# Softmax maxima from one-bank score pieces with the mask in the product, and the last output projections moved behind attention

## The chip, the cores and the metric

The kernel runs on one core of a Trainium2 chip. The metric is the device time of one launch in microseconds (us), lower is better. The engines are PE (TensorE, matmuls), DVE (VectorE), ACT (ScalarE), POOL (GpSimd) and SP (SyncE, which only issues DMAs here).

## The reference, cut to what matters

```python
xn = layernorm(x)                                  # x: 4 x 1024 x 512
q, k, v = proj(xn, Wq, bq), proj(xn, Wk, bk), proj(xn, Wv, bv)   # 16 heads of 32
s = q @ k.T / sqrt(32)                             # per batch and head, 1024 x 1024
s = where(key > query, -inf, s) - slope[h] * |key - query|
attn = softmax(s) @ v;   out1 = attn @ Wo.T + bo
g, u = split(xn @ w1[e].T);  y = (silu(g) * u) @ w2[e].T         # 8 experts, top 2 of each token
return x + out1 + moe(y, softmax gate weights)
```

## The kernel before, in words

A function `plan()` writes out by hand one order of steps (`o.steps`). Every engine's program runs through that list and emits its own steps, so each engine works its part strictly in that order, and semaphores order the engines among each other.

Attention runs over 16 groups (`G`), a batch times four heads each, and 40 units (`u`) in a group. A unit is one head's scores for 256 queries and up to 256 keys: matmuls at L1248 to L1253, kept transposed (keys on partitions) in one of two PSUM banks `C`, then an exponential on ACT (L1842). Four units make a quad, whose probabilities go through POOL's addition (L1946) and PE's products with V (L1266) and with ones (L1276 to L1279, the sums). A quarter `q` of the queries ends with `osb` (ACT), `fold` (a small DMA), `rcp` (DVE), `unfold` (a small DMA), `bc` (PE, L1288), `a32` (DVE) and `aT` (POOL).

The exponential needs each row's maximum beforehand. It comes from a first computation of the scores, with queries on partitions (`pre`, L1223), whose row maximum DVE takes (`mx`, L1652). There are 32 items a group, one for each 128-query tile `j` and head `h`, each 128 (j+1) keys wide. The DVE instruction adds a table `rel` (the distance, and -1e30 behind the diagonal) and reduces in one go. Items with j > 3 fill both banks A and B (1024 columns, two matmuls of up to 512 columns), the others one of A and C. The maxima are turned (`mtr`, L1235), copied (`mcp`, ACT) and written by a small DMA (`mrow`) into an extra row of the stacked operands, so that the second scores come out with the maximum subtracted. That stacked operand has 96 rows of q and k pieces (`stack`, 12 DMAs a group, L1041), 9 rows of positions (`place`) and the row of the maxima. Group G's items are placed from unit 40 G - 32 on.

Between the units `plan()` places filler with due times, for which units earn credit: projections of the next group (L1192, L1209), layer norm, the gate, and the output projections `proj_o(b, i)` (L1300, 12 matmuls of 512 columns each; 8 a batch). These used two further banks, T, in turn, whichever was free for the longest (`borrow`, `give`). The last batch's projections are placed from unit 604 on, due by unit 686 at the latest.

SP also issues the loads of the expert weights in six windows (`win`, L1126). Each waits for the buffers it overwrites; window 3 waits for the last products with V and the last sums. After unit 640 and the projections the mixture of experts follows (L1338, L1353, L1369): 71 slots of 128 tokens, the first of which needs the gate weights of windows 0 to 3.

Of the kernel before, what the change touches and what calls it, by code (L numbers as in the profile page):

```python
# [8 lines left out]
P = 128  # L9
B, S, E = 4, 1024, 512  # L10
NT = B * S // P
H, D = 16, 32
NG = 4
# [34 lines left out]
MAXIMA = ([(j, h) for j in (0, 1) for h in range(4)] + [(j + 2 * k, h) for j in (2, 3) for h in range(4) for k in (0, 1)]  # L48
          + [(j, h) for j in (6, 7) for h in range(4)])
# [3 lines left out]
C_ID, C_U, C_ONE, C_REL, C_IOTA, C_SLOPE, C_ALPHA, C_TAU, C_POS, C_END = (  # L53
    0, 128, 256, 384, 1408, 1416, 1432, 1436, 1436 + NSLOT, 1564 + NSLOT)
# [3 lines left out]
BND, SW, IW, SQ, IQ, SG, IG, CV, SQQ, CK, T0, CO, NQ = range(6, 19)  # L58
# [88 lines left out]
def plan():  # L147
# [131 lines left out]
    def maxima(n):  # L279
        G = n // 32  # L280
        j, h = MAXIMA[n % 32] if G else (n // 4, n % 4)
        key = "pre", G, j, h
        if j > 3:
            banks = ["A", "B"]
        else:
            banks = ["C"] if (G and j > 1) or h % 2 else ["A"]
        o.bank[key] = "C" if banks == ["C"] else "A"
        o.emptied[key] = [s for x in banks for s in o.tenant.get(("P", x), [])]
        add(*key)
        add("mx", G, j, h)  # L290
        for x in banks:
            o.tenant["P", x] = [("mx", G, j, h)]
        if h == 3 and j % 2:
            def row():
                take_m("mtr", G, j // 2)
                add("mtr", G, j // 2)

                def rest():
                    add("mcp", G, j // 2)
                    o.give(("mtr", G, j // 2), ("mcp", G, j // 2))  # L300
                    add("mrow", G, j // 2, sem=f"mrow{j // 2}", inc=16)

                later.append(rest)

            at(now[0] + 2, row)
# [277 lines left out]
    for cost in start:  # L583
        if cost:
# [6 lines left out]
            if i == 15:  # L591
                stack(0, 0)
                add("place", 1, sem="pos0", inc=16 * 5)
                add("otop")
# [6 lines left out]
    add("place", 2, sem="pos1", inc=16 * 5)  # L601
# [35 lines left out]
    for b in range(B):  # L637
# [23 lines left out]
    for n in range(32 * GROUPS):  # L661
        G, k = n // 32, n % 32
        due.setdefault(U0 + k // 2 if G == 0 else TG * G - 32 + k * 5 // 4, []).append(n)
# [60 lines left out]
    o.tenant["S", 0] = o.tenant["P", "A"] + o.tenant["P", "B"]  # L724
    o.tenant["S", 1] = o.tenant["C", 0] + o.tenant["C", 1]
    o.tenant["Y", 0], o.tenant["Y", 1] = o.tenant["O", 0], o.tenant["P", "C"]
# [60 lines left out]
def build(nc, ctx, T):  # L787
# [49 lines left out]
    down = sb("down", [P, 1], F32)  # L837
# [12 lines left out]
    rel = cF[:, C_REL:C_REL + S]  # L850
# [29 lines left out]
    junk, to = place(to, [P, S], F32)  # L880
# [3 lines left out]
    zeros = junk[:, 0:E]  # L884
    spill = [junk[:, k * 512:(k + 1) * 512].bitcast(BF16) for k in range(2)]
# [5 lines left out]
    mneg, to = place(to, [P, 2, 32], F32)  # L891
# [27 lines left out]
    PB = TB  # L919
    CB = [GU[1][:, 0:512], GU[1][:, 512:1024]]  # L920
    MXB = {"A": GU[0], "C": MB}
# [76 lines left out]
    def sync(sp):  # L998
        on = Once(sp)
        sp.dma_start(idh, T["cH"][:, 0:P]).then_inc(sems["csth"], 16)  # L1000
        for step in o.steps:
# [41 lines left out]
            elif kind == "place" and key[0]:  # L1043
# [8 lines left out]
            elif kind == "mrow":  # L1052
# [8 lines left out]
            elif kind == "fold":  # L1061
# [3 lines left out]
            elif kind == "unfold":  # L1065
# [33 lines left out]
            elif kind == "win":  # L1099
# [15 lines left out]
                elif key[0] == 4:  # L1115
                    on.wait_ge(*at("mx", GROUPS - 1, 7, 3))
# [17 lines left out]
    def tensor(pe):  # L1134
        on = Once(pe)
        reg = {}
        for step in o.steps:
# [76 lines left out]
            elif kind == "pre":  # L1214
                G, j, h = key
                w = P * (j + 1)
                z = MXB[o.bank[step]]
                for s in o.emptied[step]:
                    on.wait_ge(*at(*s))
                on.wait_ge(*at("stack", G // NG, G % NG, h))  # L1220
                for n0 in range(0, w, 512):
                    n1 = min(w, n0 + 512)
                    tp = pe.matmul(z[:, n0:n1], stk[G % 2][0:96, h, 0, j * P:(j + 1) * P], stk[G % 2][0:96, h, 1, n0:n1],  # L1223
                                   start=True, stop=True)
                tp.then_inc(sems["pre"], 1)
            elif kind == "mtr":
# [4 lines left out]
                for j in (2 * q, 2 * q + 1):  # L1231
                    for h in range(4):
                        on.wait_ge(*at("mx", G, j, h))
                for j in range(2):
                    tp = pe.transpose(z[0:4, j * P:(j + 1) * P], mneg[:, G % 2, 8 * q + 4 * j:8 * q + 4 * j + 4], idf)  # L1235
# [140 lines left out]
    def vector(dve):  # L1376
# [135 lines left out]
        then(dve.memset(down[:, :], -MDOWN))  # L1512
        for step in o.steps:
# [67 lines left out]
            elif kind == "scales" and key[0] == 4:  # L1581
                scales(MG, SG, IG, -80)
                then(dve.tensor_scalar(col(T0), col(SQQ), col(SQ), None, ALU.mult))
# [4 lines left out]
                then(dve.tensor_scalar(sel, sel, col(SQ), None, ALU.mult))  # L1588
                dve.tensor_scalar(rel, rel, col(T0), None, ALU.mult).then_inc(sems["scales"], 1)
# [51 lines left out]
            elif kind == "mx":  # L1641
                G, j, h = key
                w, m = P * (j + 1), 4 * j + h
                if G > 1:
                    on.wait_ge(*at("mtr", G - 2, j // 2))
                elif G == 0:
# [460 lines left out]
```

## Time and profile before

| | |
|---|---|
| median of 3 runs | 1655.44 us (1653.47 to 4988.74) |
| the profiled execution | 1652.5 us, of which the span of its instructions is 1650.7 us |
| granted PE clock, mean | 0.954 of full |
| PE busy | 1454.1 us, 88% |
| DVE, ACT, POOL busy | 922.4, 704.0, 875.4 us |

Busy time of PE tells when it had something in flight, not at what rate. The line PEclk of the page is the clock that PE was granted, in tenths of full speed. Times of rows are counted from the span's start. A bracket at a row's end is idle time of the engine just ahead of it, and what ended it.

### The profile page before, as it was taken

Reading aid. Unit: us, or ns where it says so; the run is one execution under the profiler, and the core shown is the slowest. Engines: PE = TensorE matmul, PEld = TensorE weight load, DVE = VectorE, ACT = ScalarE, POOL = GpSimd, SP = SyncE. Lnnn points to the kernel's source line nnn. Section 1 sums busy time; section 2 is a strip of 40 time slices with the busy share of each in tenths; the row PEclk is TensorE's granted clock in tenths of the full one; section 3 lists DMA queues with packets and bytes.
Section 4 is the critical chain, followed back from the end, with each engine's and each line's share of the span. In section 5 each row is a group of like instructions: output and inputs, shape, how many; then the busy total and the mean of one; then the engine's idle time right before and its main releaser. Section 6 shows DMA issues by size and latency. Waiting matters only on the chain. (4 is left out here: it accounts for less than half of the span.)

```text
span 1650.7 us, 35380 instructions
## 1 busy us (share of the span) xinstructions
PE 1454.1 (88%) x13147; PEld 845.5 (51%) x13147; DVE 922.4 (56%) x2128; ACT 704.0 (43%) x1179; POOL 875.4 (53%) x756
## 2 busy tenths in 40 slices
PE   4779988888997889998889889897579999999995
PEld 2345545454553554555555455553246655566663
DVE  7656775665667556657568886762134333333332
ACT  5134555444565554655655434354212222222221
POOL 4124446345356553645546535555425777767774
PEclk9789989999999999999899999998889999999997
DMA  7233541426433245433242511105786888888894
GB/s 256 64 86 105 154 129 56 116 74 178 124 120 91 87 142 156 130 108 107 74 113 84 152 28 32 40 2 186 233 252 102 135 134 137 130 121 138 142 145 49
DMA packets 189366, 194.45 MB, mean 118 GB/s; under 512 B 104953, under 2 KB 139001, under 8 KB 189074
## 3 DMA queue, kind: packets, MB, share of 16 engines
q1 hardware_dynamic: 161778, 152.84, 34.7%
q0 software_dynamic: 26128, 37.24, 13.7%
q8 instruction: 112, 1.84, 0.5%
q10 hardware_dynamic: 1296, 2.11, 0.3%
q14 instruction: 52, 0.43, 0.1%
HBM read 93.66 MB, written 53.74 MB: 89 GB/s over the span
## 5 line engine op out<-in xcount | busy, mean ns | idle before, releaser
L1842 ACT ACTIVATE arena<-S,psl 128x512 f32<-128x512 f32 (+1 forms) x640 | 403.4, 643 | 420.8 <-PE S L1250 215.4
L1652 DVE CUSTOM_DVE_ANT_0 arena<-S,cF,down 128x768 bf16<-128x768 f32 (+6 forms) x324 | 306.2, 945 | 203.5 <-PE S L1223 161.7
L1946 POOL TENSOR_TENSOR arena<-arena 128x1024 f32<-128x1024 f32 (+1 forms) x160 | 316.2, 1977 | 168.8 <-ACT arena L1842 168.6
L2000 POOL DMA_INDIRECT out<-arena x142 | 221.9, 1563 | 107.0 <-ACT arena L1895 49.6
L1338 PE MATMUL S<-arena 128*128 x1704 | 265.7, 312 | 1.2 <-issue 1.2
L1223 PE MATMUL S<-arena 96*128 96x512 f16 (+2 forms) x580 | 159.3, 348 | 76.1 <-DVE arena L1652 74.0
L1338 PEld LDWEIGHTS S<-arena 128*128 128x128 f16 x1704 | 166.3, 98 | 97.5 <-issue 2.0
L1192 PE MATMUL T<-arena 128*128 128x512 f16 x768 | 203.6, 393 | 2.0 <-DVE arena L1568 0.8
L1248 PE MATMUL S<-arena 106*128 106x256 f16 x640 | 179.9, 282 | 13.3 <-ACT arena L1842 12.7
L1266 PE MATMUL O<-arena 128*32 128x256 f32 (+1 forms) x2560 | 165.3, 378 | 0.5
L1652 DVE CUSTOM_DVE_ANT_0 arena<-M,cF,down 128x384 bf16<-128x384 f32 (+3 forms) x188 | 110.8, 589 | 90.6 <-PE M L1223 80.9
L1935 POOL TENSOR_TENSOR arena<-arena 128x512 f16<-128x512 f32 x64 | 77.3, 1208 | 142.5 <-DVE arena L1623 138.6
L1761 DVE COPY arena<-T 128x512 f16<-128x512 f16 x71 | 30.2, 425 | 213.7 <-PE T L1353 198.5
L1879 ACT ACTIVATE arena<-S,sc 128x352 f32<-128x352 f32 x71 | 39.4, 555 | 210.9 <-PE S L1338 192.0
L1266 PEld LDWEIGHTS O<-arena 128*32 128x32 f32 x2560 | 80.0, 115 | 66.5 <-issue 23.2
L1223 PEld LDWEIGHTS S<-arena 96*128 96x128 f16 x580 | 44.8, 99 | 134.4 <-DVE arena L1652 108.6
L1209 PE MATMUL T<-arena 128*128 128x128 f16 x1536 | 107.4, 221 | 6.3 <-DVE arena L1636 5.2
L1192 PEld LDWEIGHTS T<-arena 128*128 128x128 f16 x768 | 73.2, 100 | 75.2 <-issue 12.7
L1209 PEld LDWEIGHTS T<-arena 128*128 128x128 f16 x1536 | 96.2, 99 | 22.4 <-DVE arena L1636 8.0
L1956 POOL CAST arena<-arena 128x256 f16<-128x256 f32 x64 | 27.7, 433 | 148.3 <-DVE arena L1662 148.3
L1250 PE MATMUL S<-arena 106*128 106x256 f16 x384 | 104.8, 275 | 0.0
L1300 PE MATMUL T<-arena 128*128 128x512 f16 x384 | 100.7, 389 | 3.8 <-ACT arena L1849 2.0
(182 smaller groups left out, 2167.9 us busy)
## 6 DMA issues: line engine op xcount, KB each, us to landing
arena<-arena SPq DMA_DIRECT2D x192, 128.0 KB, 2.4
arena<-in_w1T SPq DMA_DIRECT2D x64, 352.0 KB, 3.5
arena<-in_x SPq DMA_DIRECT2D x64, 256.0 KB, 3.8
w_d<-arena SPq DMA_DIRECT2D x32, 352.0 KB, 2.8
arena<-w_d SPq DMA_DIRECT2D x16, 704.0 KB, 6.7
arena<-in_w2T SPq DMA_DIRECT2D x32, 256.0 KB, 3.0
out<-arena SPq DMA_DIRECT2D x32, 256.0 KB, 2.5
xn_d<-arena SPq DMA_DIRECT2D x24, 256.0 KB, 2.2
```

The costliest lines, as they stand in the source:

```text
L1192: tp = pe.matmul(z[:, :], wqkv[:, w_, c, f:f + P], xnT[:, a, c, half * 512:half * 512 + 512], start=(third == 0 and c == 0), stop=(third = ...
L1209: tp = pe.matmul(z[:, i * P:(i + 1) * P], xnT[:, a, c, k * P:(k + 1) * P], wqkv[:, w_, c, 2 * E + g * P:2 * E + (g + 1) * P], start=(n == ...
L1223: tp = pe.matmul(z[:, n0:n1], stk[G % 2][0:96, h, 0, j * P:(j + 1) * P], stk[G % 2][0:96, h, 1, n0:n1], start=True, stop=True)
L1248: pe.matmul(z[:, 0:2 * P], K[0], stk[G % 2][0:KROWS, h, 0, q0:q2], start=True, stop=False)
L1250: tp = pe.matmul(z[:, 2 * P:4 * P], K[1], stk[G % 2][0:KROWS, h, 0, q0:q2], start=False, stop=True)
L1266: tp = pe.matmul(OB[D * x:D * x + D, f:f + n], V[(G + 1) % 3][:, 2 * i + k, x * D:(x + 1) * D], PT[t % 3][:, x, c:c + n], start=(i == 0 an ...
L1300: tp = pe.matmul(z[:, :], aT[:, a, c, i * P:(i + 1) * P], wo[:, w_, c, :], start=(third == 0 and c == 0), stop=(third == 2 and c == 3))
L1338: tp = pe.matmul(y[:, i * 512:i * 512 + I], xT[:, s % XDEEP, 4 * a + c, :], weights[:, bass.ds(reg[s] + (w_ * NX * W1N + c * 2 * I + i * I ...
L1652: dve.tensor_tensor_reduce(spill[k % 2][:, 0:w], MXB[o.bank["pre", G, j, h]][:, 0:w], rel[:, S - w:S], down[:, 0:1], 3.0e38, ALU.add, ALU.min,
L1842: act.activation(PT[t % 3][:, h, 0:n], CB[o.bank["score", u]][:, 0:n], ACT.Exp, scale=psl[:, hh:hh + 1]).then_inc(sems["exp"], 1)
L1946: pool.tensor_tensor(PS[t % 2][:, :, f:f + n], PT[t % 3][:, :, f:f + n], PT[t % 3][:, :, c:c + n], ALU.add).then_inc(sems["add"], 1)
L2000: pool.indirect_dma_start(out=halves, out_offset=bass.IndirectOffsetOnAxis(row[:, part, s:s + 1].bitcast(U32), 0), in_=yo[:, s % YDEEP, c0 ...
```

## The change

The first scores are cut into 38 pieces a group, each of at most 512 columns (one bank): one head's tile over up to 512 keys, or the same stretch of two or four heads side by side. They come from the same pool as all other short-lived PSUM tenants, which now has five banks. The product now takes in the 9 rows of positions (105 rows), so that the distance is in it; pieces that reach the diagonal get one more matmul, 128 columns a head, which adds -2^30 behind the diagonal. DVE takes plain maxima over a piece of up to four heads; for j > 3 the second part is joined to the first. Items of group G are placed one a unit, from unit 40 G - 32 on. `rel` and its scaling go, and the constants shrink by 1024 columns.

The 8 output projections of the last batch are placed from unit 640 on. `place` is 2 DMAs instead of 5. In the last group `mrow`, `fold` and `unfold` are issued by ACT instead of SP.

```diff
+PIECES = [(0, (0, 1, 2, 3), 0, P), (1, (0, 1), 0, 2 * P), (1, (2, 3), 0, 2 * P)]
+PIECES += [(j, (h,), 0, P * (j + 1)) for j in (2, 3) for h in range(4)]
+for j in range(4, 8):
+    PIECES += [(j, (h,), 0, 4 * P) for h in range(4)]
+    n = 4 if j == 4 else 2 if j == 5 else 1
+    PIECES += [(j, tuple(range(h, h + n)), 4 * P, P * (j + 1)) for h in range(0, 4, n)]
...
-        self.since, self.owner = dict.fromkeys(range(2), 0), {}
+        self.since, self.owner = dict.fromkeys(range(5), 0), {}
...
     def maxima(n):
+        G, k = n // len(PIECES), n % len(PIECES)
+        key = "pre", G, k
+        take_m(*key)
         add(*key)
+        def rest():
+            add("mx", G, k)
+            o.give(key, ("mx", G, k))
+            if k == LAST[q]:
+                if q > 1:
+                    add("join", G, q, sem="mx")
+                at(now[0] + 1, row)
+        later.append(rest)
...
-            fill.append((first + k, last + (8, 18, 30, 46)[i // 2], proj_o(b, i)))
+            if b == B - 1:
+                fill.append((NU, NU + 2 * i, proj_o(b, i)))
+            else:
+                fill.append((first + k, last + (8, 18, 30, 46)[i // 2], proj_o(b, i)))
...
-        due.setdefault(U0 + k // 2 if G == 0 else TG * G - 32 + k * 5 // 4, []).append(n)
+        due.setdefault((U0 + k // 2 if k > 2 else U0) if G == 0 else TG * G - 32 + k, []).append(n)
...
+    PB = [*TB, GU[0][:, 0:512], GU[0][:, 512:1024], MB]
...
-                for h in range(4):
-                    sp.dma_start(stk[k][96:96 + NPOS, h, :, :],
-                                 posh.rearrange("p (s n) -> p s n", s=2)).then_inc(sems[f"pos{k}"], 16)
+                sp.dma_start(stk[k][96:96 + NPOS, :, :, :].rearrange("p h s n -> p h (s n)"),
+                             posh.unsqueeze(1).to_broadcast([NPOS, 4, 2 * S])).then_inc(sems[f"pos{k}"], 16)
...
             elif kind == "pre":
+                for h in heads:
+                    on.wait_ge(*at("stack", G // NG, G % NG, h))
+                on.wait_ge(*at("place", 1 + G % 2))
+                for n, h in enumerate(heads):
+                    tp = pe.matmul(z[:, n * w:(n + 1) * w], stk[G % 2][0:KROWS - 1, h, 0, j * P:(j + 1) * P],
+                                   stk[G % 2][0:KROWS - 1, h, 1, k0:k1], start=(n == 0), stop=not diagonal)
+                if diagonal:
+                    tp = pe.matmul(y[:, :, w - P:w], late[:, 0:P], big.unsqueeze(1).to_broadcast([P, len(heads), P]),
+                                   start=False, stop=True)
...
-                dve.tensor_tensor_reduce(spill[k % 2][:, 0:w], MXB[o.bank["pre", G, j, h]][:, 0:w], rel[:, S - w:S],
-                                         down[:, 0:1], 3.0e38, ALU.add, ALU.min,
-                                         mneg[:, G % 2, m:m + 1]).then_inc(sems["mx"], 1)
+                dve.tensor_reduce(d[:, heads[0]:heads[-1] + 1], z, AX, ALU.max).then_inc(sems["mx"], 1)
...
-            elif kind == "unfold":
+            elif kind == "unfold" and key[0] < GROUPS - 1:
...
+            elif kind == "unfold" and key[0] == GROUPS - 1:
+                on.wait_ge(*at("rcp", G, q))
+                act.dma_start(rrow[0:P:D, q % 2, :], rc[:, 1, q % 2, :]).then_inc(sems[f"unfold{q % 2}"], 16)
```

## Rows read from the trace of the kernel before

**Rows 1.** By stage: length, busy us (and instructions), granted clock, DMA share, GB/s.
```profile
core 0: us, PE busy (x) PEld busy (x) DVE busy (x) ACT busy (x) POOL busy (x), PEclk, DMA share, GB/s
...
49.00:108.00 59.00, 40.44 (x189) 17.47 (x189) 35.24 (x83) 11.04 (x17) 6.37 (x6) 0.71 0.29 66
108.00:1110.00 1002.00, 899.78 (x9408) 525.28 (x9405) 673.78 (x1571) 520.57 (x867) 512.12 (x462) 0.97 0.35 101
1110.00:1213.00 103.00, 68.16 (x575) 32.97 (x574) 20.16 (x40) 31.40 (x53) 46.74 (x40) 0.83 0.60 209
```
**Rows 2.** The page's groups: busy, mean ns, idle before and its releaser.
```profile
L1652 DVE CUSTOM_DVE_ANT_0 arena<-S,cF,down 128x768 bf16<-128x768 f32 (+6 forms) x324 | 306.2, 945 | 203.5 <-PE S L1223 161.7
...
L1223 PE MATMUL S<-arena 96*128 96x512 f16 (+2 forms) x580 | 159.3, 348 | 76.1 <-DVE arena L1652 74.0
...
L1248 PE MATMUL S<-arena 106*128 106x256 f16 x640 | 179.9, 282 | 13.3 <-ACT arena L1842 12.7
...
L1652 DVE CUSTOM_DVE_ANT_0 arena<-M,cF,down 128x384 bf16<-128x384 f32 (+3 forms) x188 | 110.8, 589 | 90.6 <-PE M L1223 80.9
```
**Rows 3.** Timeline of PE near 100 us: start, us, instruction.
```profile
101.58 1.03 PE L1223 MATMUL S<-arena 96*128 96x512 f16 x2 [0.49 <-DVE arena L1652]
104.00 1.03 PE L1223 MATMUL S<-arena 96*128 96x512 f16 x2 [1.39 <-DVE arena L1652]
```
**Rows 4.** Timeline of DVE, the same place.
```profile
102.65 1.28 DVE L1652 CUSTOM_DVE_ANT_0 arena<-S,cF,down 128x1024 bf16<-128x1024 f32 x1 [1.13 <-PE S L1223]
```
**Rows 5.** Groups by shape on DVE, busy and mean ns.
```profile
L1652 DVE DVE_READ_ACCUMULATOR2_ANT arena<- 128x1 f32 x512 | 42.5, 83 | 0.0
...
L1675 DVE TENSOR_REDUCE mcol<-arena 128x1 f32<-128x512 f32 x16 | 10.8, 678 | 0.9 <-DMA arena<-in_w2T 0.9
```
**Rows 6.** Timeline of PE: the masked scores of one unit.
```profile
1148.45 0.27 PE L1253 MATMUL S<-arena 128*128 128x256 f16 x1
1148.56 0.27 PE L1248 MATMUL S<-arena 106*128 106x256 f16 x1
```
**Rows 7.** What PE waited for, 0 to 60 us.
```profile
PE M L1223 <- DMA arena<-arena: 3.4, 2, 1.7
PE S L1223 <- DMA arena<-arena: 1.6, 2, 1.1
```
**Rows 8.** Timeline of PE: the first item of all.
```profile
49.91 0.23 PE L1223 MATMUL S<-arena 96*128 96x128 f16 x1 [1.12 <-DMA arena<-arena]
```
**Rows 9.** SP's issues near 50 us: the first stack and the places.
```profile
46.11 7.82 SPq L1041 DMA_DIRECT2D arena<-arena  x12
53.98 3.10 SPq L1049 DMA_DIRECT2D arena<-arena  x4
```
**Rows 10.** The page's DMA issues: stack DMAs, with the median us to landing.
```profile
arena<-arena SPq DMA_DIRECT2D x192, 128.0 KB, 2.4
```
**Rows 11.** SP's issue of the stack of group G = 4.
```profile
302.98 7.79 SPq L1041 DMA_DIRECT2D arena<-arena  x12
```
**Rows 12.** Timeline of PE: the first item of group G = 4.
```profile
313.69 0.22 PE L1223 MATMUL S<-arena 96*128 96x128 f16 x1
```
**Rows 13.** Two stretches of 20 us, columns as in rows 1.
```profile
210.00:230.00 20.00, 15.27 (x127) 7.24 (x120) 16.31 (x34) 7.33 (x14) 10.31 (x19) 0.77 0.39 111
...
410.00:430.00 20.00, 20.00 (x210) 11.87 (x207) 13.12 (x28) 13.22 (x20) 11.79 (x9) 1.00 0.35 110
```
**Rows 14.** Timeline of PE at the end of attention.
```profile
1173.24 1.19 PE L1288 MATMUL T<-arena 128*128 128x256 f32 x2 [5.05 <-DMA arena<-arena]
...
1202.34 1.19 PE L1288 MATMUL T<-arena 128*128 128x256 f32 x2 [16.91 <-DMA arena<-arena]
1205.26 8.07 PE L1300 MATMUL T<-arena 128*128 128x512 f16 x24 [1.73 <-POOL arena L1957]
```
**Rows 15.** SP's issues there: transposes, window 3, the last unfold.
```profile
1161.02 7.03 SPq L1132 DMA_TRANSPOSE arena<-arena  x4
...
1185.90 4.57 SPq L1126 DMA_DIRECT2D arena<-w_d  x9
...
1191.00 0.56 SPq L1069 DMA_DIRECT2D arena<-arena  x1
```

More of the change, by code:

```diff
@@ L279, in maxima, with row, turned_ @@
     def maxima(n):
[L280 to L288, printed above, removed]
-        add(*key)
[L290 to L305, printed above, removed]
+        G, k = n // len(PIECES), n % len(PIECES)
+        q = PIECES[k][0] // 2
+        key = "pre", G, k
+        take_m(*key)
+        add(*key)
+        def rest():
[5 more added lines that the diff above has]
+                at(now[0] + 1, row)
+        def row():
+            take_m("mtr", G, q)
+            add("mtr", G, q)
+            def turned_():
+                add("mcp", G, q)
+                o.give(("mtr", G, q), ("mcp", G, q))
+                add("mrow", G, q, sem=f"mrow{q}", inc=16)
+            later.append(turned_)
+        later.append(rest)
     def score(u):
@@ L592, in plan @@
                 stack(0, 0)
-                add("place", 1, sem="pos0", inc=16 * 5)
+                add("place", 1, sem="pos0", inc=16 * 2)
                 add("otop")
@@ L600, in plan @@
     add("wql", 6)
-    add("place", 2, sem="pos1", inc=16 * 5)
+    add("place", 2, sem="pos1", inc=16 * 2)
     assert not events and not later
@@ L660, in plan @@
     due = {}
-    for n in range(32 * GROUPS):
-        G, k = n // 32, n % 32
-        due.setdefault(U0 + k // 2 if G == 0 else TG * G - 32 + k * 5 // 4, []).append(n)
+    for n in range(len(PIECES) * GROUPS):
+        G, k = divmod(n, len(PIECES))
+        due.setdefault((U0 + k // 2 if k > 2 else U0) if G == 0 else TG * G - 32 + k, []).append(n)
     credit = 0.0
@@ L849, in build @@
     ones = cF[:, C_ONE:C_ONE + D]
-    rel = cF[:, C_REL:C_REL + S]
     to = 0
@@ L879, in build @@
     AFTER_PT = to
-    junk, to = place(to, [P, S], F32)
+    zeros, to = place(to, [P, E], F32)
     V1, to = place(to, [P, 8, P], F32)
@@ L890, in build @@
     rrow, to = place(to, [P, 2, 2 * P], F32)
-    mneg, to = place(to, [P, 2, 32], F32)
+    mpos, to = place(to, [P, 2, 32], F32)
+    mpart, to = place(to, [P, 2, 16], F32)
     mrow, to = place(to, [P, 2, 2 * P], F16)
@@ L1060, in sync @@
                              mrow[0:4, q % 2, :]).then_inc(sems[f"mrow{q}"], 16)
-            elif kind == "fold":
+            elif kind == "fold" and key[0] < GROUPS - 1:
                 G, q = key
@@ L1214, in tensor @@
             elif kind == "pre":
-                G, j, h = key
-                w = P * (j + 1)
-                z = MXB[o.bank[step]]
+                G, k = key
+                j, heads, k0, k1 = PIECES[k]
+                z, w = PB[o.bank[step]], k1 - k0
                 for s in o.emptied[step]:
                     on.wait_ge(*at(*s))
[L1220 to L1224, printed above, removed]
+                for h in heads:
+                    on.wait_ge(*at("stack", G // NG, G % NG, h))
+                on.wait_ge(*at("place", 1 + G % 2))
+                diagonal = k1 == P * (j + 1)
+                for n, h in enumerate(heads):
+                    tp = pe.matmul(z[:, n * w:(n + 1) * w], stk[G % 2][0:KROWS - 1, h, 0, j * P:(j + 1) * P],
+                                   stk[G % 2][0:KROWS - 1, h, 1, k0:k1], start=(n == 0), stop=not diagonal)
+                if diagonal:
+                    y = z[:, 0:len(heads) * w].rearrange("p (a n) -> p a n", a=len(heads))
+                    on.wait_ge(sems["cst"], 64)
+                    tp = pe.matmul(y[:, :, w - P:w], late[:, 0:P], big.unsqueeze(1).to_broadcast([P, len(heads), P]),
+                                   start=False, stop=True)
                 tp.then_inc(sems["pre"], 1)
```

68 lines of the change are left out of this document (36 added, 32 removed).

## The prediction

> **What bounds the kernel now.** I read the stages first. From 108 to 1110 us PE is busy 90% of the time, DVE 67%, ACT 52%, POOL 51% [rows 1]. PE is the bound, and there are two ways to gain: PE's idle time and PE's clock. PE's idle times in the three stages of attention are 59.0 - 40.4 = 18.6, 1002 - 899.8 = 102.2 and 103 - 68.2 = 34.8 us [rows 1]. The stage of the experts, after 1213 us, is not touched but for its start. Next, what ended PE's idle time: DVE's maxima end 74.0 us of it, ahead of the first scores, and this is the largest single cause; exponentials (ACT) end 12.7 us [rows 2]. The timeline shows how such a wait comes about. Items of 1024 columns follow each other at 101.58 and 104.00 us. Between them lie DVE's 1.28 us over both banks, the read of the accumulator and the latencies, and PE is idle for 1.39 us [rows 3, 4]. There is one pair of banks, so the next item can't start before the last is reduced. It is a wait for a buffer: DVE itself is idle 1.13 us before the reduction. The third place is the end of attention, where PE waits 5.05 and 16.91 us for `bc` and 1.73 us for `aT` [rows 14].
>
> **The change part by part.** The sum is made against the profiled execution, 1652.5 us (span 1650.7). The median of the runs, 1655.4, is 2.9 above it; I add that at the end.
>
> *Waits for maxima.* With 5 banks taken in turn and one piece a unit, a bank comes back after several units; the attention's 640 units take about 1.7 us each (1110 us over 640). A reduction of 512 elements took 678 ns, though from SBUF [rows 5]; DVE has one such piece to take off a bank in every 1.7 us. So of 74 us I let 4 stay: -70. What is late next is ACT's exponential, which the same PE order reaches sooner: I let its 12.7 us grow by half, +6.
>
> *DVE's work* costs nothing on the path while DVE has slack, but must be sized. Before: 306.2 + 110.8 = 417 us in 324 + 188 = 512 instructions [rows 2], plus 42.5 us of accumulator reads [rows 5]. After: 480 pieces of 512 elements and 128 of 384, 608 in all, at most 678 ns each: 412 us, and 32 joins of some 0.2 us, 6 us. That is 40 us less. A plain reduction from PSUM is not in this trace at this size; the other bound is the old instruction itself with its accumulator read. Its mean from banks S, 945 ns, is for 768 columns or so; a column costs about 1 ns, so that for 512 it took some 700 + 83, at most 830 ns. 608 x 830 is 505 us, 46 more than before, and DVE's share in the long stage some 72%. Even that is no bound. I take 678, since it is the same operation on as many elements. The Trainium skill speaks against this part: "VectorE: DVE Perf Modes", section Rules for kernel authors, calls the plain reduction the slowest DVE operation on a hot path and asks for fewer operations, and the change makes 96 more. The rows here price it below what it replaces [rows 2, 5], so it enters no term. By the page's rule alone the sum would lose nothing either, as long as DVE is not the bound.
>
> *Masks in the product.* 128 query tiles, 8 in each of 16 groups, get 4 heads x 128 more columns: 16 x 8 x 512 = 65,536 columns. A masking matmul of 256 columns holds PE 0.11 us, from one start to the next [rows 6]. 256 of these are 28 us. A few run at half clock, so +30. The more rows in the product (105 for 96) cost nothing, as the second scores have 106 and run 256 columns in the same 0.11 us. Splitting the rest adds no columns.
>
> *Start.* The first item needed one head's stack; now the first piece needs four heads and the place. The 12 stack DMAs are issued from 46.11 to 53.93 us, then come the place's, 0.65 us each or somewhat more, now 2: 55.3 us [rows 9]. With 2.4 us to land [rows 10] PE can go on at 57.7. PE has nothing left from 49.91 - 1.12 = 48.8 us on [rows 8], so it waits 8.9 us where it waited 3.4 + 1.6 = 5.0 [rows 7]: +4. That later places and the row of the maxima come some 4 us earlier on SP's queue is worth nothing, since they are not waited for yet.
>
> *Start of each later group.* There too the first piece, eight units behind the release of the stack, needs all four heads. For G = 4 the issues end at 310.8 us, so the last head lands at some 313.2, and PE reached the first item at 313.69 [rows 10 to 12]. So counted for each of the 15 groups, the slack runs from -0.2 to 10.5 us, and in three it is 1 us or less. Eight units shorten by 5%, 0.7 us. Price: up to 1.5 us in three groups, 0 in most, +3. Behind PE's wait stand scores of the group before, whose exponentials wait in turn.
>
> *Clock.* The stage at 49 us was granted 0.71, the long one 0.97, the tail 0.83 [rows 1]. The levels are 1.2 and 2.4 GHz, so lost at full rate are 0.29 x 59 = 17, 0.03 x 1002 = 30 and 0.17 x 103 = 18 us. The stretch at 210 us, with 4.7 us of idle time in 20, had 0.77; the one at 410 us with none had 1.00 [rows 13]. At 104 us, behind the waits, two matmuls of 512 columns are at the lower level [rows 3]. If half of the drops in the long stage go with their waits, that is -15. At the start the longer first wait speaks against a gain: 0.
>
> *Tail.* Fold and unfold stand in SP's queue behind transposes that wait for gathers, 7.03 us, and behind window 3, 4.57 us of issues; the unfold issued at 1191.00 was landed 11.2 us later, behind that window's data [rows 14, 15]. ACT now issues them directly. And six projections, 6 x 12 matmuls of 512 columns, 0.22 us each by the pace of rows 6, 15.6 us, that lay before the last sums now lie where PE waited. Of 5.05 + 16.91 + 1.73 = 23.7 us all is covered, and the 24 matmuls at 1205 us, 8.07 us, run in 5.1 at full clock [rows 14]: -23.7 - 3. Against it: ACT's in-order queue now holds an unfold that waits for DVE's reciprocal, and with it for the fold's landing (2.4 us), with exponentials behind it; about 1 us each in three quarters. And the last 36 units lose their filler, so that exponentials and POOL's additions show between them: +3. Together -21. What is late next is window 3, needed by the first expert matmul. It waits for the last sums, which in the new order stand behind two projections; 15 us of projections follow. Its data were in at the latest when the unfold behind them landed, at 1202.2 us, 16.3 us after its first issue at 1185.90 [rows 15]; the gate weights are the first two thirds, some 11 us. It is just covered.
>
> *No cost:* the constants (the scaling of `rel` was a short operation of DVE before the first projections were ready), `mcp`'s scale, the smaller tables.
>
> Sum: -70 + 6 + 30 + 4 + 3 - 15 - 21 = -63. 1652.5 - 63 = 1589.5, with 2.9 for the median 1592 us.
>
> **The rivals.**
>
> *A, the waits change their cause.* The PE order is fixed, and other engines' work is bound to it. If only half of the 70 us goes (DVE's queue also has casts, splits of the expert weights and routing, and is at 67% [rows 1]) and the clock gives back 5 us instead of 15: 1592 + 35 + 10 = 1637 us, within 2%. For it: 12.7 us of waits for exponentials already. Against it: DVE sits idle before the reduction [rows 4]. Chance 0.20.
>
> *B, slower: the stack.* The first piece of every group stops PE until the fourth head has landed. The price is at most the three later heads' issues, 9 of 12 parts of 7.8 us, 5.9 us and their delayed followers, some 7.5 us, in 15 groups, 112 us: 1592 - 3 + 112 = 1701 us. It decides from where the eight units between release and first piece take less than 10.3 us; they took 10.7 us for G = 4 [rows 11, 12] and 11 to 21 in the others, and only a gain larger than mine would shorten these so far. Chance 0.03.
>
> *C, the clock comes back wholly.* Without waits the long stage runs like that at 410 us [rows 13]: 15 us more, and the waits for exponentials don't grow: 1592 - 21 = 1571 us. Chance 0.15.
>
> *D, the tail gives nothing.* The change would then not do what it says there. If the small DMAs on ACT's queue land as late as before, 11.2 us, PE reaches `bc` some 6 us of projections behind the last sums and waits another 8 us: 1600 us. This is also what the Trainium skill's "DMA: Bandwidth & Descriptors", section Issuing engines are not separate DMA queues, would have: all queues run on the same DMA engines, and another issuer saves only issue time. No row here shows a small transfer on ACT's queue under this load. Chance 0.15.
>
> **How the numbers follow.** The forecast, with terms each off by a few us, 1580 to 1610: 0.47. A change of 2% or more (below 1622 or above 1689 us) is about what a measurement of this kernel can tell from none. Faster by that: the forecast, C, D and a third of A, 0.83; within 2%: 0.14; slower: 0.03. The range goes from C's lower side, 1562, to 1630, which leaves out B and half of A.
>
> **What would show it.** The row of L1223's matmuls should have lost its 74 us of idle time to DVE, with no other row gaining over 20. The matmuls of that step are 70 instead of 48 a group. Plain reductions should be at 600 to 700 ns for 512 elements. PE's busy share in the long stage should be near 95% and its clock 0.98 or more. At the first piece of group 0 a wait of 8 to 9 us for DMA. The last unfold landing in 3 to 5 us, projections back to back, and attention's end at about 1150 us. The prediction is wrong if the waits return under another name (ACT, POOL or the stack), if a reduction from PSUM takes a microsecond, or if the first expert matmul waits for window 3.

## The result and the profile after

The changed kernel takes 1605.7 us (median of 4 runs, 1602.3 to 1609.7) where the kernel before takes 1654.5 us beside it: ratio 0.972, 95% interval 0.968 to 0.977. One of the four runs of the kernel before took 4988.7 us and is left out of the ratio. Run again later it took 1599.8 us, ratio 0.970 [0.967, 0.972]. The middle of the two, 0.971, is the reference below. The effect of an experiment is its own ratio less 0.971, times 1652 us, known to about 4 us either way; where the changed kernel ran beside it on the same chip, that comparison is given. The profiled execution went from a span of 1650.7 to one of 1600.5 us, 50.2 less: 43.5 us of PE's idle time (196.6 to 153.1) and 6.7 us of its busy time (1454.1 to 1447.4).

The stages after, columns as in [rows 1]:
```profile
core 0: us, PE busy (x) PEld busy (x) DVE busy (x) ACT busy (x) POOL busy (x), PEclk, DMA share, GB/s
...
49.00:108.00 59.00, 42.55 (x361) 25.72 (x362) 37.37 (x69) 16.79 (x28) 9.55 (x7) 0.86 0.35 84
108.00:1070.00 962.00, 895.44 (x9588) 542.05 (x9589) 650.33 (x1209) 516.78 (x859) 512.37 (x460) 0.98 0.36 104
1070.00:1162.00 92.00, 66.57 (x574) 31.80 (x574) 16.03 (x31) 30.94 (x52) 46.70 (x40) 0.85 0.65 226
```
The long stage is 962 us instead of 1002, 93% busy instead of 90%, at 0.98 instead of 0.97. The stretch at 49 us has 0.86 instead of 0.71. Attention ends at 1161.8 us, where it ended at 1213.

The page's groups after, for [rows 2]:
```profile
L1658 DVE TENSOR_REDUCE arena<-T 128x1 f32<-128x512 f32 (+3 forms) x241 | 156.2, 654 | 92.7 <-PE T L1236 53.7
L1658 DVE TENSOR_REDUCE arena<-S 128x1 f32<-128x512 f32 (+3 forms) x256 | 167.0, 657 | 72.3 <-PE S L1236 39.3
L1259 PE MATMUL S<-arena 106*128 106x256 f16 x640 | 178.5, 279 | 27.5 <-ACT arena L1851 27.0
...
L1231 PE MATMUL T<-arena 105*128 105x512 f16 (+3 forms) x293 | 91.1, 341 | 19.9 <-DMA arena<-in_up 10.2
...
L1231 PE MATMUL S<-arena 105*128 105x512 f16 (+3 forms) x338 | 96.8, 327 | 3.5 <-DMA arena<-arena 3.3
...
L1658 DVE TENSOR_REDUCE arena<-M 128x1 f32<-128x512 f32 (+3 forms) x111 | 73.2, 660 | 34.8 <-PE M L1231 23.4
```
The first scores' matmuls (L1231) have lost their 74 us of waits for DVE; of their idle time what is left ends mostly with DMAs. The exponentials' waits (L1259) have doubled. The maxima take DVE 156.2 + 167.0 + 73.2 = 396 us, where they took 306.2 + 110.8 + 42.5 = 459.5. Two shapes of the reduction, from PSUM (columns: busy, mean ns):
```profile
L1658 DVE TENSOR_REDUCE arena<-T 128x1 f32<-128x512 f32 x156 | 106.2, 685 | 54.7 <-PE T L1231 38.0 <-PE T L1236 16.1
...
L1658 DVE TENSOR_REDUCE arena<-T 128x1 f32<-128x384 f32 x55 | 30.2, 551 | 22.8 <-PE T L1236 22.6
```
and the old instruction at 512 columns, in the kernel before:
```profile
L1652 DVE CUSTOM_DVE_ANT_0 arena<-M,cF,down 128x512 bf16<-128x512 f32 x62 | 46.4, 748 | 24.2 <-PE M L1223 23.8
```
With its accumulator read, 83 ns [rows 5], that is 831 ns against 685. At 1024 columns the old one took 1282 + 83 ns, as much as two plain pieces. So DVE's time fell by the narrow items, which are now reduced for two or four heads in one instruction.

What PE waited for in the whole span (us in total, times, longest), the rows that concern the change:
```profile
...
PE T L1299 <- DMA arena<-arena: 9.2, 4, 7.6
PE S L1299 <- DMA arena<-arena: 8.1, 2, 7.6
PE T L1231 <- DMA arena<-arena: 8.0, 2, 6.0
...
PE S L1246 <- DVE arena L1658: 5.0, 4, 4.0
PE T L1246 <- DVE arena L1663: 4.2, 2, 3.8
PE M L1299 <- DMA arena<-arena: 3.4, 5, 1.2
PE S L1231 <- DMA arena<-arena: 3.3, 3, 1.5
...
PE T L1231 <- DVE arena L1658: 1.7, 2, 1.4
PE M L1231 <- DVE arena L1658: 1.6, 2, 1.4
```
L1246 is the transposition of the maxima's rows (`mtr`), L1663 the join of a tile's two partial maxima on DVE, L1299 the matmul of `bc`.

The start, and the start of group 1, on PE's timeline; and SP's issues ahead of the first:
```profile
57.09 0.58 PE L1231 MATMUL T<-arena 105*128 105x128 f16 x4 [10.24 <-DMA arena<-in_up]
...
95.90 0.59 PE L1231 MATMUL T<-arena 105*128 105x128 f16 x4 [6.03 <-DMA arena<-arena]
```
```profile
44.17 7.82 SPq L1047 DMA_DIRECT2D arena<-arena  x12
...
52.97 0.67 SPq L1056 DMA_DIRECT2D arena<-in_up  x1
```
The end of attention, on PE, on ACT's and SP's queues, and on POOL:
```profile
1147.85 1.19 PE L1299 MATMUL S<-arena 128*128 128x256 f32 x2 [7.64 <-DMA arena<-arena]
...
1154.55 2.76 PE L1311 MATMUL T<-arena 128*128 128x512 f16 x12 [1.02 <-POOL arena L1982]
...
1161.77 7.33 PE L1349 MATMUL S<-arena 128*128 x48 [1.86 <-DVE arena L1678]
```
```profile
1136.89 0.56 ACTq L1874 DMA_DIRECT2D arena<-arena  x1
```
```profile
1135.38 4.41 SPq L1132 DMA_DIRECT2D arena<-w_d  x9
1139.84 0.44 SPq L1083 DMA_DIRECT2D arena<-in_x  x1
```
```profile
1152.13 1.27 POOL L1988 TENSOR_TENSOR arena<-arena 128x512 f32<-128x512 f32 x1 [13.19 <-DMA arena<-in_x]
```
The last unfold is issued by ACT at once, at 1136.89 us, and PE still can't use it before 1147.85, 11.0 us later: it was issued 1.5 us after the first of window 3's nine loads. The load of the last residual tile, issued behind that window at 1139.84, lands about 12 us later too, and POOL waits for it.

### The profile page after: what moved, and what is told of

Same layout as the page of the kernel before. It is cut to its first block, busy times and chain, and to the rows that moved or that the text cites. A ratio compares the mean times of both kernels' runs of the same rounds, so it can differ in the third digit from the quotient of the medians.

```text
span 1600.5 us, 35240 instructions
## 1 busy us (share of the span) xinstructions
PE 1447.4 (90%) x13499; PEld 868.3 (54%) x13499; DVE 897.5 (56%) x1741; ACT 705.4 (44%) x1179; POOL 878.1 (55%) x756
## 4 chain that ended last, share of the span: by engine, by line
PE 66%; DVE 8%; POOL 7%; SPq 6%; DMA 6%; issue 4%; ACT 2%; ACTq 0%; POOLq 0%; DVEq 0%
PE S L1349 16%; PE O L1277 6%; SPq L1047 5%; PE S L1198 4%; PE O L1380 4%; PE M L1380 4%; DVE arena L1658 3%; PE S L1259 3%; PE T L1215 3%; PE T L1198 3%; PE O L1287 3%; PE T L1231 2%; PE S L1231 2%; DMA arena<-in_x 2%; POOL arena L1971 2%
## 5 line engine op out<-in xcount | busy, mean ns | idle before, releaser
L1658 DVE TENSOR_REDUCE arena<-T 128x1 f32<-128x512 f32 (+3 forms) x241 | 156.2, 654 | 92.7 <-PE T L1236 53.7
L1658 DVE TENSOR_REDUCE arena<-S 128x1 f32<-128x512 f32 (+3 forms) x256 | 167.0, 657 | 72.3 <-PE S L1236 39.3
L1259 PE MATMUL S<-arena 106*128 106x256 f16 x640 | 178.5, 279 | 27.5 <-ACT arena L1851 27.0
L1259 PEld LDWEIGHTS S<-arena 106*128 106x128 f16 x640 | 63.4, 99 | 85.6 <-ACT arena L1851 45.6
L1231 PE MATMUL T<-arena 105*128 105x512 f16 (+3 forms) x293 | 91.1, 341 | 19.9 <-DMA arena<-in_up 10.2
L1198 PE MATMUL S<-arena 128*128 128x512 f16 x408 | 104.8, 383 | 0.9 <-DVE arena L1578 0.6
L1231 PE MATMUL S<-arena 105*128 105x512 f16 (+3 forms) x338 | 96.8, 327 | 3.5 <-DMA arena<-arena 3.3
L1988 POOL TENSOR_TENSOR arena<-arena 128x512 f32<-128x512 f32 x32 | 41.9, 1320 | 101.9 <-DMA arena<-in_x 101.9
L2012 POOL DMA_INDIRECT arena<-xn_d,tl x71 | 72.5, 1022 | 40.9 <-DMA arena<-arena 19.6
L1658 DVE TENSOR_REDUCE arena<-M 128x1 f32<-128x512 f32 (+3 forms) x111 | 73.2, 660 | 34.8 <-PE M L1231 23.4
L1712 DVE SCALAR_TENSOR_TENSOR arena<-arena,sc 128x704 f16<-128x704 f32 (+2 forms) x56 | 69.2, 1235 | 31.7 <-ACT arena L1893 31.7
```

The source lines that it names most:

```text
L1198: tp = pe.matmul(z[:, :], wqkv[:, w_, c, f:f + P], xnT[:, a, c, half * 512:half * 512 + 512], start=(third == 0 and c == 0), stop=(third = ...
L1231: tp = pe.matmul(z[:, n * w:(n + 1) * w], stk[G % 2][0:KROWS - 1, h, 0, j * P:(j + 1) * P], stk[G % 2][0:KROWS - 1, h, 1, k0:k1], start=(n ...
L1259: pe.matmul(z[:, 0:2 * P], K[0], stk[G % 2][0:KROWS, h, 0, q0:q2], start=True, stop=False)
L1658: dve.tensor_reduce(d[:, heads[0]:heads[-1] + 1], z, AX, ALU.max).then_inc(sems["mx"], 1)
```

## The experiments

**Again.** The changed kernel itself, run beside the second group of experiments.

> The changed kernel itself, as the base for the three kernels run with it: 1603 to 1608 us, a ratio of 0.972 to the kernel before.

1599.8 us against 1650.8; ratio 0.970 [0.967, 0.972].

**1. How many banks the pool has.** (Two later lines that name banks 3 and 4 are adapted.)
```
-        self.since, self.owner = dict.fromkeys(range(5), 0), {}
+        self.since, self.owner = dict.fromkeys(range(3), 0), {}
```


> The changed kernel with 3 banks in the pool instead of 5, same pieces and same places in the order. Theory 1 (the gain is the number of banks: a buffer comes back several units later): matmuls of the first scores and projections wait for DVE and ACT again, 15 to 40 us more, 1620 to 1645 us. Rival (small pieces alone make the gain, a reduction of 0.69 us is over before its bank is wanted): 1600 to 1612 us, no row of waits for DVE over 10 us.

1642.9 us, ratio 0.995 [0.993, 0.997]: 40 us over the changed kernel. Nearly all of the gain is gone, although the pieces, the reductions and the masks are the same. The waits of PE:
```profile
PE T L1231 <- DVE arena L1658: 10.2, 20, 1.1
PE T L1231 <- ACT arena L1858: 8.1, 3, 3.5
```
Waits of about half a us per piece for DVE are back, with one for ACT's copy of the rows, which now holds one bank of three. But at the pieces they come to 13.7 us (10.2 and 3.5), where the kernel before had 77. The idle time is 18 us above the changed kernel's (171.1), and the busy time 22 us above with the same matmuls at nearly the same clock (0.963). So more than half of the price lies in busy records, and its form stays open.

What this shows is that three banks are too few for this order: the other two are worth 40 us. It doesn't show which part of the change made the gain. The kernel before had the same five banks, two as T and three for the maxima (A, B and the one beside them), so none was added. They were put into one pool, and each item now needs one bank where the wide ones needed A and B together. The small pieces with the banks divided as before were not run, nor was the old reduction in the pool.

**2. The masks' columns, doubled.** Each masking matmul of the first scores is issued twice.
```
-                    tp = pe.matmul(y[:, :, w - P:w], late[:, 0:P], big..., start=False, stop=True)
+                    for last in (False, True):
+                        tp = pe.matmul(y[:, :, w - P:w], late[:, 0:P], big..., start=False, stop=last)
```


> The changed kernel with each masking matmul of the first scores issued twice. Theory 1 (PE is the bound and pays each column): +28 us, 1634 us. Rival (a good part of the columns lies in waits for the exponentials, 27 us, and for DMAs): +8 to +15 us, 1614 to 1621 us.

1620.0 us, ratio 0.981 [0.978, 0.985]: 17 us over the changed kernel. PE's busy time grew by 25 us (1472.5), its idle time fell by 7 (146.5). 28 us of columns cost 17, and 7 us of the rest took the place of waits.

**3. The tail alone, on the kernel before.** The last batch's projections from the end of the scores, and the last group's small transfers on ACT's queue; first scores and maxima as before.
```
+            if b == B - 1:
+                fill.append((NU, NU + 2 * i, proj_o(b, i)))
...
+            elif kind == "unfold" and key[0] == GROUPS - 1:
...
+                act.dma_start(rrow[0:P:D, q % 2, :], rc[:, 1, q % 2, :]).then_inc(sems[f"unfold{q % 2}"], 16)
...
```


> The kernel before with only the end of attention changed: the last batch's projections placed from unit 640, and the last group's small DMAs issued by ACT. By the prediction's term -21 us: 1633 us. By what the trace after shows (new waits of 7.6 us for bc, 1.0 and 1.9 us behind the load of the residual, window loads over everything): -5 to -12 us, 1642 to 1649 us.

1645.7 us, ratio 0.996 [0.993, 0.998]: 7 us less, a third of the tail's 21 us in the prediction. Its last `bc` waits 7.45 us; there were 16.91 [rows 14]. The experts start at 1205.6 us instead of 1213.2.

**4. The small transfers back on SP's queue**, in the changed kernel (the last group's row, fold and unfold).
```
...
-            elif kind == "unfold" and key[0] < GROUPS - 1:
+            elif kind == "unfold":
...
```


> The changed kernel with the last group's row, fold and unfold DMAs issued by SP again. Theory 1 (the DMA engines set the landing, 10.9 us on ACT's queue after against 11.2 on SP's before, so that the issuer only saves the 4.4 us of window 3's issues ahead of the last unfold and SP's other waits): +3 to +8 us, 1609 to 1614 us. Rival (the issuer is worth nothing since PE waits for the residual's load through POOL anyway): within 2 us of 1605.7.

1612.9 us, ratio 0.977 [0.974, 0.980]: 10 us over the changed kernel. The timeline of PE at the last `bc`, and SP's queue:
```profile
1170.07 1.19 PE L1299 MATMUL S<-arena 128*128 128x256 f32 x2 [12.42 <-DMA arena<-arena]
```
```profile
1153.06 4.54 SPq L1132 DMA_DIRECT2D arena<-w_d  x9
...
1158.62 0.55 SPq L1074 DMA_DIRECT2D arena<-arena  x1
```
The unfold is issued behind the window, 4.5 us of issues, and needs 11.5 us to be used, as on ACT's queue (11.0). The other queue saves the issues ahead of it and nothing of the data.

**5. Every group's pieces 3 units later.**
```
-... else TG * G - 32 + k, []).append(n)
+... else TG * G - 29 + k, []).append(n)
```


> The changed kernel with every group's pieces three units later (from unit 40 G - 29). Theory (the first piece of a group waits for the fourth head's stack, 12 us in all, 6.0 us of it in group 1): those waits for DMA under 2 us, and 8 to 12 us less time, 1594 to 1598 us. Rival (a wait that goes here comes back at the next exponential or at the row of maxima, since the engines are bound to one order): 1602 to 1606 us, with more idle time at the scores.

1616.5 us, ratio 0.981 [0.978, 0.984], 17 us more than the changed kernel beside it. Neither theory had that. The waits for the stacks did go (2.3 us left at L1231), but others came:
```profile
PE S L1246 <- DVE arena L1663: 14.8, 4, 5.0
PE M L1311 <- POOL arena L1982: 12.2, 1, 12.2
...
PE T L1246 <- DVE arena L1663: 8.5, 5, 4.7
PE M L1246 <- DVE arena L1663: 8.0, 4, 2.5
```
The first of these waits, on DVE's, POOL's and PE's timelines:
```profile
161.21 2.12 DVE L1663 TENSOR_TENSOR arena<-arena 128x8 f32<-128x8 f32 x1
```
```profile
160.98 2.34 POOL L1971 TENSOR_TENSOR arena<-arena 128x1024 f32<-128x1024 f32 x1
```
```profile
163.48 0.58 PE L1246 MATMUL S<-cF,arena 128*4 128x128 f32 x2 [4.99 <-DVE arena L1663]
```
A join of 8 columns takes 2.12 us where 0.17 is usual, and it ends with POOL's addition (163.33 and 163.32). Of the 32 joins 13 take over 0.5 us, up to 2.29, and eleven of these are seen to end within 0.03 us of an instruction of POOL; in the changed kernel one join is that long, 2.21 us. The 32 take 19.9 us instead of 7.6, and PE stands behind them, 31.3 us in all. The idle time is then the same as in the changed kernel beside it (150.1 and 151.3 us); the busy time is 10 us longer at the lower mean clock, 0.954 instead of 0.962. The two profiled executions differ by 9 us only, so the trace shows half of the 17, and that half is clock. PE's listed waits are 66 of 131.7 us in all, where there were 87 of 133.4; that fewer and longer waits lower the clock was not tested by itself.

**6. The second place ahead of the first stack.**
```
+                add("place", 1, sem="pos0", inc=16 * 2)
                 stack(0, 0)
-                add("place", 1, sem="pos0", inc=16 * 2)
```


> The changed kernel with the first place's two DMAs issued ahead of the first stack. Theory (the first piece waits for them last: 10.2 us for the DMA from in_up): the wait becomes one for the fourth head's stack, about 7.5 to 9 us, 1.5 to 2.7 us less time, 1603 to 1604 us. Rival: no difference, since the 12 stack DMAs are issued that much later: 1606 us.

1598.9 us, ratio 0.971 [0.967, 0.974]: no difference to the changed kernel beside it (1599.8).
```profile
54.00 0.59 PE L1231 MATMUL T<-arena 105*128 105x128 f16 x4 [7.07 <-DMA arena<-arena]
```
The first piece waits 7.07 us instead of 10.24, and 3 us are too little for this measurement.

**7. The transposition of the rows two units behind the last maximum instead of one.**
```
-                at(now[0] + 1, row)
+                at(now[0] + 2, row)
```


> The changed kernel with the turning of the maxima (mtr) two units behind the quarter's last maxima instead of one. Theory (PE waits 11.8 us for DVE's maxima and joins at mtr, where it waited 4.6 us before the change): under 3 us of such waits, 5 to 9 us less time, 1597 to 1601 us. Rival (DVE is then late for other reasons and PE waits a unit later): 1604 to 1606 us.

1605.1 us, ratio 0.974 [0.971, 0.977], 5 us more than the changed kernel beside it. The waits of `mtr` for DVE fell from 11.8 to 3.4 us, and in the tail the cause of a wait moved:
```profile
1139.03 0.67 PE L1299 MATMUL S<-arena 128*128 128x256 f32 x2 [1.62 <-DMA arena<-arena]
1153.84 4.96 PE L1311 MATMUL T<-arena 128*128 128x512 f16 x12 [10.68 <-POOL arena L1982]
1163.31 7.43 PE L1349 MATMUL S<-arena 128*128 x48 [1.91 <-issue]
```
The unfold was issued at 1134.10 us, 0.03 us ahead of the window's first load, and `bc` came 4.9 us later. But POOL stood 13.68 us at the residual's addition, with `aT` behind it in its queue, so the experts started at 1163.3, no earlier than in the changed kernel.

**8. Window 3 six units later.**
```
-    for u, k in (..., (NU + 6, 3), (NU + 15, 4)):
+    for u, k in (..., (NU + 12, 3), (NU + 15, 4)):
```


> The changed kernel, with the fourth window of expert weights (9 loads of 512 KB in all with its neighbours, issued by SyncE just before the last small transfer) asked for 6 units later. In the changed kernel the last rescaling row is asked for at 1136.9 us and its matmul starts at 1147.9 us after 7.6 us of waiting; the residual of the last projection tile, issued behind the same window, holds GpSimd for 13.2 us. Theory: both small transfers are late because the window's data are ahead of them, not because of the queue they were issued on. Then the wait of the last rescaling matmul falls from 7.6 to under 3 us, GpSimd's wait from 13.2 to about 5 us, and the experts' first matmul comes 5 to 8 us earlier: 5 to 8 us less in all, unless the later window is then waited for by the experts. Rival: the time of a small transfer is its own and stays near 10 us; nothing changes (within 3 us).

1607.9 us, ratio 0.973 [0.970, 0.975]: 3 us over the reference, no difference.
```profile
1139.89 0.59 PE L1299 MATMUL S<-arena 128*128 128x256 f32 x2
...
1156.18 8.77 PE L1349 MATMUL S<-arena 128*128 x48 [7.07 <-issue]
...
1180.06 5.20 PE L1349 MATMUL S<-arena 128*128 x24 [6.77 <-DMA arena<-arena]
```
Issued at 1136.73, the unfold is used at 1139.89 without a wait: 3.2 us at most instead of 11.0, on the same queue. It was the window's data that held it. The experts start 5.6 us earlier, though, and then wait for what was put off: 7.07 us ahead of their first matmul and 6.77 us ahead of a later one. The profile names no releaser for the first of the two. Window 3's first load was issued 16.5 us before that matmul, and the last projection's copy was long done, so I take it for the window. In experiment 10 it was 16.6 us.

**9. The last residual's addition behind `aT` on POOL.**
```
-        add("xbo", b, i)
+        if (b, i) != (B - 1, 7):
+            add("xbo", b, i)
...
                 add("aT", G, q)
+                if (G, q) == (GROUPS - 1, 3):
+                    add("xbo", B - 1, 7)
```


> The changed kernel, with GpSimd's addition of the residual of the last projection tile moved behind the transposed copy that the last two projections read. Theory: in the changed kernel that copy stands in GpSimd's queue behind an addition which waits 13.2 us for a load, 1 to 4 us longer than the copy's own operand needs; moving it brings the copy to within 1 us of its operand and saves 1 to 4 us, if the last tile's store is not what is late then. Rival: the copy is held by the rescaling matmul alone, and nothing changes (within 1.5 us).

1601.1 us, ratio 0.968 [0.966, 0.971]: 4 us under the reference, at the edge of what can be told.
```profile
1148.19 0.40 POOL L1984 CAST arena<-arena 128x256 f16<-128x256 f32 x1 [10.53 <-DVE arena L1674]
```
(L1984 is what L1981 was: the edit adds three lines.) POOL now waits for `aT`'s own operand and makes it at once; the projections follow `bc` without the 1.02 us. But from `bc` to the experts' first matmul it is 13.7 us (1146.48 to 1160.16) where it was 13.9, so the trace credits the edit with 0.2 us and not with 4.

**10. Edits 6, 8 and 9 together.**

> The three small edits together: the fourth window 6 units later, GpSimd's last residual addition behind the transposed copy, and the second placing of queries ahead of the first stack. Theory: 6 to 10 us less than the changed kernel (ratio to the kernel before about 0.964 where the changed kernel has 0.970 to 0.972). Rival: the end of attention is held by the chain through the last product, its row sums and two small transfers, whose own latencies stay; then 0 to 3 us less.

1603.5 us, ratio 0.970 [0.968, 0.972]: no gain over the changed kernel. The last projections end at 1146 us, and the experts' first matmul comes at 1153.16 us after 7.12 us of waiting; from there to the end it takes 444.2 us, where the changed kernel takes 438.7. What the tail gains, the put-off window takes.

**11. The last batch's projections where they stood before**, in the changed kernel.
```
-            if b == B - 1:
-                fill.append((NU, NU + 2 * i, proj_o(b, i)))
-            else:
-                fill.append((first + k, last + (8, 18, 30, 46)[i // 2], proj_o(b, i)))
+            fill.append((first + k, last + (8, 18, 30, 46)[i // 2], proj_o(b, i)))
```


> The changed kernel, with the eight output projections of the last batch (192 matmuls, about 44 us of TensorE) put back to where they stood before, two to three triples ahead of the end as soon as their operands are ready; the small transfers stay on ScalarE's queue. If the projections do cover waits at the end of attention, as the prediction's tail term says, this kernel is 12 to 20 us slower than the changed one (ratio to the kernel before 0.980 to 0.983), with waits of 5 to 8 us for transfers back in front of the last rescaling matmuls. Rival, from the small gain of the tail edits when they stood alone: the projections give TensorE other gaps to fill inside attention, where it waits for exponentials, so it is 0 to 6 us slower (0.970 to 0.975).

1615.9 us, ratio 0.978 [0.975, 0.980]: 11 us over the reference (9 and 13 over the two runs of the changed kernel), between the two expectations.
```profile
1167.41 1.19 PE L1296 MATMUL T<-arena 128*128 128x256 f32 x2 [16.77 <-DMA arena<-arena]
```
The wait of 16.91 us of [rows 14] is back at full length (16.77), as is the one of 1.73 for POOL (1.72). ACT issues both small transfers itself here, too:
```profile
1150.46 0.56 ACTq L1867 DMA_DIRECT2D arena<-arena  x1
1161.65 0.55 ACTq L1871 DMA_DIRECT2D arena<-arena  x1
```
The unfold (L1871) follows the fold (L1867) after 11.2 us, where the changed kernel takes 2.9 (1133.98 to 1136.89 us). The fold was issued 0.6 us behind window 3's first load (1149.82) here, so the transfer that meets the bulk data first pays 11 us; the unfold behind it took 5.8 more until `bc`. Work in front of the wait covers this.

## Why the prediction held, and where it didn't

The forecast was 1592 us, and the two medians of the changed kernel are 1605.7 and 1599.8: inside the range and inside the likeliest case's 1580 to 1610, 8 to 14 us above the value. The bound was named rightly. That the number is so near owes something to luck: the terms below are off by 39 us one way and 21 the other. The sum's terms, against the profiled execution:

*Waits for maxima, -70.* The rows at the pieces went from 77.0 (74.0 and 3.0) to 3.6 us (1.7 + 1.6, and 0.3 in the group of S): -73. With three banks they are still only 13.7 us (experiment 1), so most of this row went with the narrow pieces and the common pool together, which no run separates; the two further banks took off the last 10 us, and 40 us of time. But `mtr`, which draws on the same chain, was left out of the sum: its waits went from 4.6 to 11.8 us, +7. Experiment 7 removes most of them without a gain.

*Exponentials, +6.* They went from 12.7 to 27.0 us: +14. This is rival A's mechanism: with `mtr` 15 us over my terms, where A had 35 (and 10 of clock).

*DVE's work at no cost.* Held: 396 us where 412 were reckoned, with 685 ns for 512 elements from PSUM against 678 from SBUF [rows 5]. The Trainium skill, "VectorE: DVE Perf Modes", section Rules for kernel authors, calls this the slowest operation of DVE; on scores in PSUM it was the cheaper of the two here (685 ns against 748 + 83 at 512 columns).

*Masks, +30.* 28 us of columns. When they are doubled, the time grows by 17 us, PE's busy time by 25. If the first 28 us behave like the second, the term was some 13 us too dear.

*Start, +4, and the later groups' stacks, +3.* These were too small. The first piece waits 10.2 us where 8.9 were reckoned. The rest is in the pieces of the groups: 8.0 + 3.3 + 0.9 = 12.2 us, of which 6.03 at group 1 alone. Together 22.4 against 5.0, +17 instead of +7. The step that failed is that the slack of every group was read off the trace of before, less 0.7 us (5% of eight units). The stack's issue and the first item of group 1, before:
```profile
96.81 7.82 SPq L1041 DMA_DIRECT2D arena<-arena  x12
...
109.35 0.22 PE L1223 MATMUL S<-arena 96*128 96x128 f16 x1
```
and the stack's issue after:
```profile
86.11 7.80 SPq L1047 DMA_DIRECT2D arena<-arena  x12
```
From the first issue to PE's arrival it was 12.5 us, and now it is 3.8 (to 89.87, which is 95.90 less the wait). Over the 15 groups it fell from 15.4 to 12.3 us on average. In these eight units lay six of the widest items of the group before, whose waits are gone; the 5% are an average. In group 1 these waits were 3.6 us, and what else shortened the stretch is open. In six groups the stretch is now under the 10.3 us from which rival B was to start, which it had called out of reach. So B's mechanism came, at 12 us instead of 112.

Experiment 5 takes these waits away, and the pieces then collide with other work of DVE and POOL: the slack can't be bought by shifting alone.

*Clock, -15.* Span times one less the mean clock was 76 us (0.954) and is 56 (0.965): -20. By the rounded clocks of the stages some 9 us of it lie in the stretch at 49 us, which was priced at 0, and some 11 in the long one, where 15 were expected. PE's busy time should then have changed by 28 - 20 = +8 us and did so by -6.7. The other 15 us stay open. Records of pipelined matmuls overlap [rows 6], and even 28 us of added columns showed as 25 in experiment 2, so a sum of busy times resolves no better than some us.

*Tail, -21.* This is the term that was mis-sized. The waits of `bc` fell from 28.1 to 20.7 us, 7 instead of 22, and attention ended at 1161.8 us instead of 1150. Alone on the kernel before the tail gives 7 us (experiment 3). In the changed kernel, taking out either half costs about 10 (experiments 4 and 11), which suggests that neither half works without the other: projections cover the wait if they lie right in front of it, and the transfer must be issued early. What both are worth in the changed kernel together was not measured. The failing step is "the last unfold landing in 3 to 5 us": it took 11.0, behind window 3's data, which is the mechanism of rival D at its size (11.2). D priced it at 8 us, and the term fell short by 14. By the Trainium skill, "DMA: Bandwidth & Descriptors", section Issuing engines are not separate DMA queues, transfers of all issuers interleave on the same engines, and another issuer saves its issue time alone; the traces agree: 11.5 us on SP's queue (experiment 4), 11.0 on ACT's (the changed kernel), at most 3.2 on ACT's with the window behind it (experiment 8). The other half of the step, that window 3 is just covered, held only because attention ended late. Its gate weights were reckoned at 11 us from the first issue, and experiments 8 and 10 show 16.5 and 16.6 us to the first expert matmul. From 1135.38 us that is 1151.9, behind the 1150 of the forecast. Nothing is left to put off (experiments 8 and 10), and the 7 us only change their name: unfold, residual or window.

Of the idle time's -43.5 us these rows give -73 + 7 + 14 + 17 - 7 = -42. Against the sum, too cheap were `mtr` (7), the exponentials (8), the stacks (10) and the tail (14); too dear the masks (13), the clock (5) and the maxima (3): 18 us more in all. The profiled execution came out 13 above the sum (1602.3 against 1589.5), and the other 5 us are not accounted for.

Of what was to be seen, this came: no other row gained over 20 us, the reductions are at 685 ns, the clock is 0.98, and the matmuls of L1231 and the masks' L1236 are 70 a group (768 + 352 in 16 groups). This did not: PE is 93% busy instead of 95, the first piece waits 10.2 us instead of 8 to 9, the last unfold did not land in 3 to 5 us, the projections are not back to back, and attention ends at 1162 us instead of 1150. Of the signs of being wrong one came in part: 14 us of the waits returned at the exponentials, 12 at the stacks and 7 at `mtr`.

## What to carry to other kernels

When an engine waits a little before each of many items and the engine that frees the buffer is itself idle, count buffers before work, and look whether those that are there can be shared in smaller pieces: one more instruction a piece is cheap beside a bank that is free. A wait that is removed brings every transfer that was just in time before into view, and the slack must be worked out from the new pace at that place, not from the old trace and a mean. At a hand-over between stages look at what bulk loads stand ahead of a small transfer; another queue doesn't pass them, independent work put right before the wait covers it, and here putting the loads off only moved the wait.

## What the runs showed of the hardware

A plain maximum over PSUM took 685 ns for 512 elements and 551 for 384: 1.05 ns an element and some 150 ns fixed, the same whether one, two or four results come out of 512 (685, 681 and 685 ns). The fused reduction that it replaced took 748 ns and 83 for its accumulator read at 512 columns, and 1282 and 83 at 1024. A DVE operation on two SBUF operands of 8 columns took up to 2.29 us instead of 0.17 while POOL ran an addition over SBUF, and ended with it (experiment 5). By the Trainium skill, "GPSIMD Engine Reference", section 1. Specifications, GpSimd and VectorE share their SBUF interfaces, with contention for VectorE instructions that have two SBUF inputs; the rows of experiment 5 agree. And 48 matmuls of the experts took 8.77 us after 7.07 us of waiting (experiment 8) but 7.33 after 1.86; the granted clock was 0.82 from 1156 to 1165 us there, and 1.00 from 1161.7 to 1169 us in the changed kernel.
